# Mamba-style block with a top-2 expert FFN on one core: the same work in another order

## The chip, the cores and the metric

The kernel runs on one core of one Trainium2 chip. The metric is the device time of one execution in microseconds (us), lower is better. The core has five in-order instruction queues that matter here: TensorE (PE, with its weight loads PEld), VectorE (DVE), ScalarE (ACT), GpSimd (POOL) and SyncE (SP), which issues nearly all DMAs. They meet only at semaphores: an instruction that waits holds all that stands behind it on its own queue.

## What is computed

Batch 4, length 1024, width 1024, all float32. First a selective-scan block over the context (512 wide) is gated by the layer-normed input z, then an FFN with two of eight small experts a batch element.

```python
# block 1, per batch element; z = layernorm(x) taken with channels as the time axis
x1  = in_proj_w @ ctx;  u = silu(causal_conv4(x1) + conv_b)
x_dbl = x_proj_w @ u                      # 32 rows dt, 16 rows B, 16 rows C
delta = softplus(dt_proj_w @ dt + dt_proj_b);  A = -exp(A_log)
state = state * exp(delta*A) + (delta*u) * B   # a scan over 1024 steps, 16 states a channel
y = (sum_n state*C + D*u) * silu(z);  x = x + y.T
# block 2, with h = layernorm(x)
logits = h.reshape(b, -1) @ switch_w.T + switch_b   # 1M x 8 weights
gate, top = top_k(softmax(logits), 2)
o = sum over the 2 experts of gate * (gelu(h @ w1.T + b1) @ w2.T + b2), in 16 heads of 64
x = x + (h + o) @ w3.T + b3
```

## The kernel before

**Tiling and stages.** Time is cut in two halves of T = 512, channels in J = 8 blocks of P = 128. A batch has STEPS = 16 steps, one for a half and a channel block, and there are NB = 4 batches, so 64 steps (g = 0 to 63). A step has SLOTS = 8 slots, and in a slot two of the N = 16 states are done: slot t of a batch is step t // 8, q = t % 8. So a batch has slots 0 to 127. After the last comes a tail of its own slots (b = NB), which holds what is left of the FFN of the last batch.

**A slot.** ScalarE makes dA = exp(delta * A) for two states (L1246, a ring of RA = 4). VectorE makes the product du * B in PSUM (times_b, L1501) and scans (L1525) into h, which has RH = 3 pairs. POOL multiplies the pair by C (L865). TensorE adds the pair into yT by transposing matmuls (sum_pair, L962). In batch 0 ten of the sixteen du * B products run on TensorE instead (times_b, L948), out of duT, which is du_s turned by turn_du (L929, at q = 7) and copied by ScalarE at q = 0 of the next step (copy_duT, L1209).

**Once a step.** For the step AHEAD = J + 2 steps on: in_proj (L900, PE, q = 6, through PSUM bank S), first tap of the convolution (tap_one, ACT, L1163 to L1172, q = 1), three taps on VectorE between scans (tap, L1357), Silu (silu_u, L1178, q = 6). For the next step: v (dt_proj, L921, PE, q = 2), softplus on ScalarE (L1190 to L1196, q = 4) and its last part on VectorE (softplus_c, L1373, q = 3), du_s on POOL (L836), its copy (copy_du, L1202, ACT, q = 7). For the gate: xz normed (L1261, ACT, q = 3), turned (zT, L1081, PE, q = 4), Silu (L1278, q = 6, szT), szT times yT (L1425), added to xt on POOL (L852), stored.

**x_proj.** It is needed once for a half. It runs in the step with st % 8 == 6, four blocks at q = 6 and four at q = 7 (x_proj and x_proj_end, L912, bank S). split_rows (ACT, L1184 and L1185) takes its rows at the start of the next step, ahead of that step's first dA. In that step in_proj runs twice (slot 0 and slot 6), and everything from tap to v is a slot later. Steps 7 and 15 are such steps (in batch 3 only step 7).

**The FFN** of batch b - 1 is laid over the scan of batch b by a hand-written plan (class Schedule): the lists `slots[b][t]` say what every engine does in slot t beside the scan. `forward` places the work: logits (L1112), routing on VectorE (route1, route2), then for each half u of the time eight units hp: hidden (L1055, PE), gelu (L1331, ACT, with a table load before and one after, L1213), expert_out (L1065, PE), out_add (L1477, DVE). Units of half 0 start at slot 39 and those of half 1 at slot 83, one in two slots. Then 32 w3 tile parts a half (L1135, PE; four parts make a tile; a bias by L1131 at its start), evenly over slots 56 to 78 and 99 to 126, and tile_out (L1489, DVE, and the store on SP) two slots behind a tile's last part. renorm (L1310) and turn (L1042) make the normed rows and their transposes.

**LN1.** The scale r1 and shift nm1 of the next batch come from ln1_stats at slots 57 to 67 (ACT, L1300 to L1304), ln1_rstd (POOL, L806) at slot 124 and ln1_shift (DVE, L1366) at slot 126. ln1_rstd waits until the last xz of its batch is normed (zn_done), since there is one copy of r1.

**The tail** needs the last rows of x1 (late_row, SP, L702), their statistics (L1443), logits out of 32 switch tiles (sw_tail, SP, L734, of which 23 are loaded in the last slots of batch 3 and after), renorm, the selection of the experts, 16 units and 64 tiles.

Of the kernel before, what the change touches and what calls it, by code (L numbers as in the profile page):

```python
# [11 lines left out]
P = 128  # L12
# [13 lines left out]
HL = DC - 1  # L26
SD = 128
# [36 lines left out]
class Schedule:  # L64
# [32 lines left out]
    def add(self, b, t, *what):  # L97
        self.slots[b][t].append(what)

    def scan(self, b, rows):  # L100
# [12 lines left out]
        if b + 1 < NB:  # L113
            for k in range(J):
                rows.append((b, 54 + 3 * k // 2, "ln1", k))
                self.add(b, 57 + 3 * k // 2, "ln1_stats", k)
            self.add(b, 124, "ln1_rstd")
            self.add(b, 126, "ln1_shift")

    def forward(self, b, rows):  # L120
# [19 lines left out]
        for u, hidden, tiles, span in ((0, 39, 56, 23), (1, 83, 99, 28)):  # L140
# [7 lines left out]
            for dh in range(NQ):  # L148
                for k in range(TB):
# [4 lines left out]
                    self.add(b, at[m + W3C - 1] + 2 if at[m + W3C - 1] < 126 else 127, "tile_out", u, dh, k)  # L154
# [8 lines left out]
    def tail(self, rows):  # L163
        b = NB

        for m in range(SWL * TB):
# [4 lines left out]
            elif m < AFTER_B:  # L171
                self.add(b - 1, 114, "sw_tail", m)
        for q in range(PAIRS):
            self.add(b - 1, 120 + q, "sw_tail", AFTER_B + q)
            self.add(b - 1 if q < PAIRS - 1 else b, (121 + q) % 128, "sw_tail", AFTER_B + PAIRS + q)
        for m in range(AFTER_B + 2 * PAIRS, SWL * TB):
            self.add(b, 0, "sw_tail", m)
        for k in range(TB):
            self.add(b - 1, 126, "late_row", k)
        for k in range(TB):  # L180
# [10 lines left out]
            self.add(b, 10 + SWL * k + 8, "renorm", k)  # L191
# [6 lines left out]
        self.add(b, 45, "route2")  # L198
        for k in range(TB):
# [14 lines left out]
        for dh in range(NQ):  # L214
            for u in (0, 1):
                for k in range(TB):
# [3 lines left out]
                    self.add(b, t, "tile_out", u, dh, k)  # L220
# [42 lines left out]
def build(nc, x, ctxT, w_inT, conv_w, conv_b, x_projT, dt_projT, dt_b, A_log, D, sw, sw_b,  # L263
# [4 lines left out]
    with ExitStack() as ctx:  # L268
# [17 lines left out]
        minus_half = sb("minus_half", [P, 1])  # L286
# [33 lines left out]
        r1 = sb("r1", [P, J])  # L320
        nm1 = sb("nm1", [P, J])
# [18 lines left out]
        b1s = sb("b1s", [P, 1])  # L340
        b2s = sb("b2s", [P, 1])
# [27 lines left out]
        wt = sww[:, 0].rearrange("p e s -> p (e s)")[:, 0:E * HD].rearrange("p (e f) -> p e f", e=E)  # L369
# [87 lines left out]
        sel_step = sem("sel_step")  # L457
        renorm_done = sem("renorm_done")
# [89 lines left out]
        def hs_of(b, hp):  # L548
            return hs_tail if b == NB and hp % 2 else hs[:]

# [12 lines left out]
        def _(sync):  # L563
# [86 lines left out]
            def slot(b, t):  # L650
# [33 lines left out]
                for what, *a in PLAN.slots[b][t]:  # L684
# [50 lines left out]
                    elif what == "sw_load":  # L735
# [43 lines left out]
                    elif what == "tile_out":  # L779
                        uu, dh, k = a  # L780
                        n = part_index(b, uu, dh, k, 0) // W3C
                        lo = half(uu) * T + k * P
                        e.wait_ge(evac[bank_of(b, "tile", uu, dh, k)], 1 + count(b, "tile", uu, dh, k) + 1)
                        e.dma_start(out[b - 1:b, lo:lo + P, dh * QD:(dh + 1) * QD]
# [861 lines left out]
```

## Time and profile before

| | |
|---|---|
| runs | 2468.3, 2472.0, 2475.0 us; median 2472.0 |
| profiled execution | 2471.2 us, span 2469.3 us |
| PE busy | 2013.5 us, 82% |
| DVE busy | 2133.6 us, 86% |
| ACT busy | 1602.4 us, 65% |
| POOL busy | 1445.2 us, 59% |

Scans run from 78.9 to 2272.2 us, 64 steps; the tail follows. Steps of batch 0 take 26.3 to 40.8 us, the longest being steps 7 and 15; steps of batches 1 to 3 take 30.3 to 43.9. Batches 1, 2 and 3 start at 561.7, 1145.3 and 1727.0 us. A step's number in the text is st, its place in its batch.

Times in rows are microseconds from the span's start. "[1.10 <-ACT u L1172]" behind an instruction says that its engine was idle for 1.10 us before it, and that this instruction of ScalarE ended the wait. "issue" is a wait for which the profile shows no releaser. Several instructions of a kind are merged in a timeline row, with the count behind x.

### The profile page before, as it was taken

What the parts mean: (1) busy time and instruction counts of PE and PEld (TensorE: products, weight loads), DVE (VectorE), ACT (ScalarE), POOL (GpSimd) and SP (SyncE); (2) the same over time, 40 slices, a digit from 0 to 9 for tenths busy, and PEclk for the clock granted to TensorE, in tenths of its full rate; (3) what the DMA queues carried; (4) which work ended last, traced back from release to release, by engine and by line L of the source; (5) the groups of instructions that cost most, each with busy time, mean ns of one, the idle gap of its engine ahead of it and who ended that gap; (6) DMA issues with size and microseconds to landing.
All of it is one profiled execution on the core that took longest, in us unless ns stands there. A gap on an engine that the chain in (4) does not pass through costs nothing.

```text
span 2469.3 us, 32717 instructions
## 1 busy us (share of the span) xinstructions
PE 2013.5 (82%) x10776; PEld 1203.1 (49%) x10776; DVE 2133.6 (86%) x2712; ACT 1602.4 (65%) x2357; POOL 1445.2 (59%) x993
## 2 busy tenths in 40 slices
PE   6798888985757997996675897898685798797899
PEld 2677676653433553454453454454453455344344
DVE  5899789979999899998999899998999899999322
ACT  2677787656669868655667878855576857954500
POOL 0588677767756566566675566665775666665000
PEclk9899889997878998997888999899787899999899
DMA  5311434555612754566542464466460174578412
GB/s 174 128 37 52 150 99 148 188 162 169 246 37 103 261 166 133 161 204 203 188 155 74 140 232 152 147 224 199 154 239 26 60 253 145 164 251 283 168 56 72
DMA packets 200329, 383.01 MB, mean 155 GB/s; under 512 B 31553, under 2 KB 97089, under 8 KB 200162
## 3 DMA queue, kind: packets, MB, share of 16 engines
q1 hardware_dynamic: 196992, 380.47, 46.1%
q8 instruction: 86, 1.41, 0.2%
q10 hardware_dynamic: 3170, 0.47, 0.1%
q14 instruction: 81, 0.66, 0.1%
HBM read 346.80 MB, written 34.08 MB: 154 GB/s over the span
## 4 chain that ended last, share of the span: by engine, by line
PE 44%; DVE 19%; issue 17%; ACT 14%; POOL 3%; DMA 1%; DVEq 0%; SPq 0%; ACTq 0%; POOLq 0%
PE dense L1135 13%; PE dense L962 9%; DVE h L1525 9%; PE dense L900 5%; ACT dA L1246 4%; PE dense L948 3%; DVE dense L1501 3%; POOL h L865 3%; DVE u L1357 2%; PE dense L912 2%; PE dense L1112 2%; ACT L1213 2%; PE dense L921 2%; PE dense L1065 2%; PE dense L969 2%
## 5 line engine op out<-in xcount | busy, mean ns | idle before, releaser
L865 POOL TENSOR_TENSOR h<-h,Cb 128x1024 f32<-128x1024 f32 x512 | 1208.4, 2361 | 431.8 <-DVE h L1525 408.2
L1246 ACT ACTIVATE dA<-delta,Av 128x512 f32<-128x512 f32 x1024 | 703.1, 717 | 384.6 <-DVE h L1525 381.3
L962 PE MATMUL dense<-ident,h 128*128 128x128 f32 x4096 | 605.4, 299 | 165.0 <-POOL h L865 163.5
L962 PEld LDWEIGHTS dense<-ident,h 128*128 128x128 f32 x4096 | 521.1, 155 | 315.6 <-POOL h L865 225.8
L1525 DVE TENSOR_TENSOR_SCAN h<-dA,state,dense 128x512 f32<-128x512 f32 x512 | 627.4, 1263 | 31.0 <-issue 14.4
L1525 DVE TENSOR_TENSOR_SCAN h<-dA,dense 128x512 f32<-128x512 f32 x512 | 596.7, 1203 | 22.0 <-PE dense L962 8.5
L1501 DVE TENSOR_TENSOR dense<-dense,Bb 128x512 f32<-128x512 f32 x864 | 550.5, 682 | 1.6
L1135 PE MATMUL dense<-w3h,xT 128*128 128x512 f32 x832 | 386.0, 598 | 0.0
L859 POOL COPY state<-h 128x2 f32<-128x2 f32 x256 | 47.6, 186 | 336.6 <-DVE h L1525 335.1
L948 PE MATMUL dense<-Bb,duT 128*128 128x128 f32 x1280 | 179.9, 289 | 41.1 <-DVE h L1525 31.7
L1135 PEld LDWEIGHTS dense<-w3h,xT 128*128 128x128 f32 x832 | 147.9, 192 | 130.1 <-issue 130.1
L900 PE MATMUL dense<-ctxs,win 128*128 128x512 f32 x432 | 208.5, 628 | 2.2 <-ACT szT L1278 1.5
L948 PEld LDWEIGHTS dense<-Bb,duT 128*128 128x128 f32 x1280 | 160.4, 199 | 72.9 <-issue 65.6
L921 PE MATMUL dense<-dtaug,dtw 33*128 33x512 f32 x128 | 95.2, 832 | 110.2 <-DVE u L1357 108.5
L1357 DVE SCALAR_TENSOR_TENSOR u<-dense,cw,u 128x511 f32<-128x511 f32 (+2 forms) x192 | 140.7, 733 | 50.6 <-ACT u L1172 24.8
L1213 ACT ACT_TABLE_LOAD x113 | 145.0, 1283 | 2.0
L900 PEld LDWEIGHTS dense<-ctxs,win 128*128 128x128 f32 x432 | 84.2, 204 | 101.8 <-issue 101.8
L1112 PE MATMUL dense<-sww,row 128*32 128x256 f32 x1336 | 110.5, 417 | 1.2 <-ACT row L1287 1.2
L1065 PE MATMUL dense<-hs,w2s 128*64 128x512 f32 x224 | 72.8, 729 | 44.0 <-ACT hs L1331 41.4
L1202 ACT COPY dense<-du_s 128x512 f32<-128x512 f32 x64 | 37.5, 587 | 103.5 <-DVE dense L1501 103.3
L921 PEld LDWEIGHTS dense<-dtaug,dtw 33*128 33x128 f32 x128 | 24.5, 239 | 140.5 <-issue 140.4
L1487 DVE TENSOR_TENSOR res<-res,h 128x512 f32<-128x512 f32 x16 | 11.1, 691 | 88.1 <-PE dense L1135 88.1
(168 smaller groups left out, 2084.1 us busy)
## 6 DMA issues: line engine op xcount, KB each, us to landing
sww<-in_sw SPq DMA_DIRECT2D x167, 512.0 KB, 4.2
Cb<-bc_scratch SPq DMA_DIRECT2D x64, 512.0 KB, 6.1
Bb<-bc_scratch SPq DMA_DIRECT2D x54, 512.0 KB, 4.6
w3h<-in_sw SPq DMA_DIRECT2D x52, 512.0 KB, 8.2
w3h<-in_w3T SPq DMA_DIRECT2D x52, 512.0 KB, 5.2
row<-x_scratch SPq DMA_DIRECT2D x40, 512.0 KB, 4.5
xz<-in_x SPq DMA_DIRECT2D x64, 256.0 KB, 4.7
xt<-in_x SPq DMA_DIRECT2D x64, 256.0 KB, 3.9
```

The costliest lines, as they stand in the source:

```text
L865: e.tensor_tensor(h[:, s:s + 2, :], h[:, s:s + 2, :], Cb[:, 2 * q:2 * q + 2, :], ALU.mult).then_inc(prod_done, 1)
L900: mm = e.matmul(dense[:, bank, :], win[:, par, k, :], ctxs[:, k, :], start=(k == 0), stop=(k == DK - 1))
L921: e.matmul(dense[:, S, :], dtw[0:DR + 1, j * P:(j + 1) * P], dtaug[:], start=True, stop=True) \
L948: mm = e.matmul(dense[:, product_bank(g, n), k * P:(k + 1) * P], duT[:, g % 2, k, :], Bb[:, n, k * P:(k + 1) * P], start=True, stop=True)
L962: mm = e.matmul(yT[:, k, :], h[:, 2 * ((PAIRS * g + q) % RH) + i, k * P:(k + 1) * P], ident[:], is_transpose=True, start=False, stop=(q == ...
L1112: mm = e.matmul(dense[32 * n:32 * n + 32, F2, 0:32 * E], rows[:, lo:lo + 32], weights[:, :, 32 * n:32 * n + 32], start=first, stop=(k % TB ...
L1135: mm = e.matmul(dense[:, bank, :], xT_of(b, uu)[:, d, k * P:(k + 1) * P], w3[:, d, :], start=(b == NB and d == 0), stop=(d == J - 1), skip ...
L1213: e.preload_act_table_set("natural_log_exp_and_others")
L1246: e.activation(dA[:, i % RA, :], delta[:, st % 2, :], ACT.Exp, scale=Av[:, j * N + n:j * N + n + 1]).then_inc(dA_done, 1)
L1357: i = e.scalar_tensor_tensor(out=u[:, G % UR, s:T], in0=dense[:, bank, 0:T - s], scalar=cw[:, j, k:k + 1], in1=u[:, G % UR, s:T], op0=ALU. ...
L1501: e.tensor_tensor(dense[:, product_bank(g, n), :], du[:], Bb[:, n, :], ALU.mult).then_inc(duB_done, 1)
L1525: e.tensor_tensor_scan(h[:, 2 * ((PAIRS * g + q) % RH) + n % 2, :], dA[:, (N * g + n) % RA, :], dense[:, product_bank(g, n), :], state[:, ...
```

## The change

Only the order of the work changes, and two small buffers.

- split_rows moves behind the first two dA and uD of its step.
- x_proj's first half waits for four of the eight u, its second half for all. On ScalarE at q = 6, Silu of szT comes ahead of Silu of u.
- In batch 0 turn_du moves from the end of q = 7 to ahead of in_proj (or x_proj) at q = 6.
- hidden and its unit move one slot later, to 40 and 84; tiles to 57 to 78 and 100 to 126. tile_out may now fall in slot 128, which is slot 0 of the next batch.
- hidden waits only for w1s, expert_out and gelu for the whole selection. In the tail the second half of w1s is made on POOL (select), in steps of its own.
- ln1_rstd and ln1_shift move to slots 69 and 71; r1 and nm1 get two buffers.
- In batch 3 late_row moves from slot 126 to 125, and the switch tiles of slots 124 and 125 to 126. In the tail renorm moves from slots 18, 26, 34 and 42 to 33, 35, 46 and 46.

The diff, cut to its core:

```diff
     def add(self, b, t, *what):
+        if b < NB and t >= STEPS * SLOTS:
+            b, t = b + 1, t - STEPS * SLOTS
         self.slots[b][t].append(what)
...
-            self.add(b, 124, "ln1_rstd")
-            self.add(b, 126, "ln1_shift")
+            self.add(b, 69, "ln1_rstd")
+            self.add(b, 71, "ln1_shift")
...
-        for u, hidden, tiles, span in ((0, 39, 56, 23), (1, 83, 99, 28)):
+        for u, hidden, tiles, span in ((0, 40, 57, 22), (1, 84, 100, 27)):
...
-                    self.add(b, at[m + W3C - 1] + 2 if at[m + W3C - 1] < 126 else 127, "tile_out", u, dh, k)
+                    self.add(b, at[m + W3C - 1] + 2, "tile_out", b, u, dh, k)
...
+        for k in range(TB):
+            self.add(b - 1, 125, "late_row", k)
         for q in range(PAIRS):
-            self.add(b - 1, 120 + q, "sw_tail", AFTER_B + q)
-            self.add(b - 1 if q < PAIRS - 1 else b, (121 + q) % 128, "sw_tail", AFTER_B + PAIRS + q)
+            for t, m in ((120 + q, q), (121 + q, PAIRS + q)):
+                t = t if t < 124 else max(t, 126)
+                self.add(b - (t < 128), t % 128, "sw_tail", AFTER_B + m)
...
-        for k in range(TB):
-            self.add(b - 1, 126, "late_row", k)
...
-            self.add(b, 10 + SWL * k + 8, "renorm", k)
+            self.add(b, (33, 35, 46, 46)[k], "renorm", k)
...
+        self.add(b, 45, "select")
...
# gpsimd, ln1_rstd
-                e.wait_ge(zn_done, 1 + STEPS * b)
+                e.wait_ge(zn_done, 1 + STEPS * max(b - 1, 0))
...
# gpsimd, in the tail
+                    elif what == "select":
+                        e.wait_ge(top_step, 1 + 9 * (b - 1) + 8)
+                        e.wait_ge(experts_loaded, 1 + 64 * b)
+                        e.tensor_tensor(wt1, w12[:, 0], hot[:, 1, :].unsqueeze(2).broadcast_to([P, E, HD]), ALU.mult) \
+                            .then_inc(w1_step, 1)
+                        for n, rest in ((1, 4), (2, 2)):
+                            e.wait_ge(w1_step, 1 + n)
+                            e.tensor_tensor(wt1[:, 0:rest], wt1[:, 0:rest], wt1[:, rest:2 * rest], ALU.add).then_inc(w1_step, 1)
+                        e.wait_ge(w1_step, 1 + 3)
+                        e.tensor_tensor(w1s[:, 1, :], wt1[:, 0], wt1[:, 1], ALU.add).then_inc(w1_step, 1)
...
# tensor
-                e.wait_ge(u_done, 1 + J * (c + 1))
+                e.wait_ge(u_done, 1 + J * c + J // 2)
...
                     times_b_at(N * g + 2 * q + 3)
+                    if q == SLOTS - 2 and g + 1 < STEPS:
+                        turn_du(g + 1)
...
-                            e.wait_ge(sel_step, 1 + 9 * b)
+                            e.wait_ge(sel_step, 1 + selected(b) + (5 if b < NB else 3))
+                            if b == NB:
+                                e.wait_ge(w1_step, 1 + 4)
...
+                        if hp == 0:
+                            e.wait_ge(sel_step, 1 + selected(b + 1))
...
                     elif what == "x_proj_end":
+                        e.wait_ge(u_done, 1 + J * (c + 2))
                         x_proj_part(c + 1, range(J // 2, J))
...
-                if b == 0 and q == SLOTS - 1 and g + 1 < STEPS:
-                    turn_du(g + 1)
...
# scalar
-                if b < NB and late(b, t, 0) and st % J == J - 1 and c + 1 < NB * TH:
-                    split_rows(c + 1)
...
                         e.activation(uD[:], u[:, g % UR, :], ACT.Copy, scale=Dv[:, j:j + 1]).then_inc(uD_done, 1)
+                        if st % J == J - 1 and c + 1 < NB * TH:
+                            split_rows(c + 1)
...
                         e.wait_ge(x1_done, 1 + g)
+                        e.wait_ge(zT_done, 1 + g + 1)
+                        e.activation(szT[:].rearrange("p k e -> p (k e)"), dense[:, S, :], ACT.Silu) \
+                            .then_inc(evac[S], 1)
...
                             silu_u(G, S, last_step(b, st, "in_proj"))
-                        e.wait_ge(zT_done, 1 + g + 1)
-                        e.activation(szT[:].rearrange("p k e -> p (k e)"), dense[:, S, :], ACT.Silu) \
-                            .then_inc(evac[S], 1)
...
# vector, route2
-                for src, on, dst in ((w12[:, 0], hot[:, 0, :], w1s[:, 0, :]), (w12[:, 0], hot[:, 1, :], w1s[:, 1, :]),
-                                     (w12[:, 1], hot[:, 3, :], w2s[:])):
+                first = [(w12[:, 0], hot[:, i, :], w1s[:, i, :]) for i in ((0,) if b == NB else (0, 1))]
+                for src, on, dst in (*first, (w12[:, 1], hot[:, 3, :], w2s[:])):
```

## Rows read from the trace of the kernel before

**Rows 1.** Windows view, core 0: start:end, length, busy us of each engine (instructions), PEclk, DMA.

```profile
733.00:770.00 37.00, 25.39 (x121) 12.72 (x118) 33.67 (x42) 34.76 (x47) 22.80 (x19) 0.91 0.29 101
845.00:881.00 36.00, 34.95 (x140) 20.81 (x139) 33.74 (x41) 30.30 (x49) 21.60 (x11) 0.95 0.79 279
1063.00:1101.00 38.00, 38.00 (x185) 19.09 (x184) 32.54 (x39) 18.29 (x28) 23.31 (x15) 1.00 0.60 204
```

**Rows 2.** Waits of VectorE, whole span: who waits for whom, total us, times, longest.

```profile
DVE delta L1373 <- ACT delta L1196: 33.0, 16, 5.1
DVE h L1525 <- issue: 20.9, 8, 5.9
DVE h L1525 <- PE dense L962: 16.9, 26, 1.8
DVE h L1525 <- ACT dA L1246: 12.5, 11, 5.6
DVE res L1489 <- PE dense L1135: 11.5, 8, 2.5
```

**Rows 3.** Waits of all engines in 130 to 270 (batch 0).

```profile
DVE u L1357 <- ACT u L1172: 5.5, 5, 1.1
ACT duT L1209 <- PE dense L929: 4.8, 5, 1.0
```

**Rows 4.** Waits of VectorE in 427 to 492 (batch 0, steps 12 to 14).

```profile
DVE u L1357 <- ACT u L1163: 5.3, 3, 1.8
```

**Rows 5.** Timeline of PE from 424 and of DVE from 425: start, duration, instruction.

```profile
425.77 1.04 PE L962 MATMUL dense<-ident,h 128*128 128x128 f32 x8
...
427.01 2.45 DVE L1525 TENSOR_TENSOR_SCAN h<-dA,state,dense 128x512 f32<-128x512 f32 x2
```

**Rows 6.** Timeline of PE from 519, and waits of PE in the whole span.

```profile
519.24 0.66 PE L929 MATMUL dense<-ident,du_s 128*128 128x128 f32 x4
...
PE dense L948 <- ACT duT L1209: 5.2, 3, 1.8
```

**Rows 7.** Timeline of 1095.4 to 1102.6 (batch 0's FFN, into step 15 of batch 1).

```profile
1099.43 0.57 ACT L1184 COPY dtaug<-dense 32x512 f32<-32x512 f32 x1 [6.72 <-PE dense L912]
1101.44 1.28 DVE L1525 TENSOR_TENSOR_SCAN h<-dA,state,dense 128x512 f32<-128x512 f32 x1 [5.87 <-issue]
```

**Rows 8.** Waits of PE in 1001.6 to 1128.4.

```profile
PE dense L921 <- DVE u L1357: 3.0, 1, 3.0
```

**Rows 9.** Waits of DVE in 733 to 770.

```profile
DVE u L1357 <- ACT u L1172: 2.1, 1, 2.1
DVE h L1525 <- PE dense L962: 0.3, 1, 0.3
```

**Rows 10.** Lines view of ACT in 733 to 809: busy us, mean ns, idle before.

```profile
L1331 ACT ACT_TABLE_LOAD x8 | 10.3, 1283 | 3.9 <-PE dense L1055 3.9
```

**Rows 11.** Timeline of PE in 803.6 to 826.

```profile
822.50 0.60 PE L1131 MATMUL dense<-ident,b3c 128*128 128x128 f32 x4
822.94 1.88 PE L1135 MATMUL dense<-w3h,xT 128*128 128x512 f32 x4
824.75 1.12 PE L921 MATMUL dense<-dtaug,dtw 33*128 33x512 f32 x2
```

**Rows 12.** Timeline of PE from 2316: the first hidden pair of the tail.

```profile
2316.61 1.22 PE L1055 MATMUL dense<-xT,w1s 64*128 64x512 f32 x2 [2.92 <-DVE b2s L1599]
```

**Rows 13.** The instructions of L1366 (durations in ns), and one in DVE's timeline from 551.

```profile
L1366 DVE SCALAR_TENSOR_TENSOR nm<-mv,r x4: 137/2300/2306, 81.1 to 1714.9; 128x8 f32<-128x8 f32 x4
...
551.34 2.30 DVE L1366 SCALAR_TENSOR_TENSOR nm<-mv,r 128x8 f32<-128x8 f32 x1 [3.39 <-POOL r L806]
```

**Rows 14.** Timelines of PE and DVE in the tail.

```profile
2274.73 1.97 PE L962 MATMUL dense<-ident,h 128*128 128x128 f32 x8 [3.76 <-POOL h L865]
...
2278.97 0.67 DVE L1425 TENSOR_TENSOR szT<-dense,szT 128x512 f32<-128x512 f32 x1
...
2298.99 1.12 PE L1042 MATMUL dense<-ident,ctxs 128*128 128x128 f32 x8 [0.77 <-ACT xT L1320]
```

More of the change, by code:

```diff
@@ L26 @@
 HL = DC - 1
+SELECT = 9
 SD = 128
@@ L219, in tail @@
                         self.add(b, t, "tile", u, dh, k, c)
-                    self.add(b, t, "tile_out", u, dh, k)
+                    self.add(b, t, "tile_out", b, u, dh, k)
                     t += 4
@@ L285, in build @@
         iota = sb("iota", [P, E])
-        minus_half = sb("minus_half", [P, 1])
+        small = sb("small", [P, 3])
+        minus_half, b1s, b2s = small[:, 0:1], small[:, 1:2], small[:, 2:3]
         xpw = sb("xpw", [P, J, DR + 2 * N])
@@ L319, in build @@
         mv1 = sb("mv1", [P, J, 2])
-        r1 = sb("r1", [P, J])
-        nm1 = sb("nm1", [P, J])
+        r1 = sb("r1", [P, 2, J])
+        nm1 = sb("nm1", [P, 2, J])
         row = sb("row", [P, 2, DI])
@@ L368, in build @@
         xT_tail = u[:, UR - J:UR, :]
-        wt = sww[:, 0].rearrange("p e s -> p (e s)")[:, 0:E * HD].rearrange("p (e f) -> p e f", e=E)
+        wt, wt1 = [sww[:, 0].rearrange("p e s -> p (e s)")[:, i * E * HD:(i + 1) * E * HD].rearrange("p (e f) -> p e f", e=E)
+                   for i in (0, 1)]
         dense = ctx.enter_context(nc.psum_tensor("dense", [P, 8, T], F32))
@@ L457, in build @@
         sel_step = sem("sel_step")
+        w1_step = sem("w1_step")
         renorm_done = sem("renorm_done")
@@ L549, in hs_of, with selected @@
             return hs_tail if b == NB and hp % 2 else hs[:]
+        def selected(b):
+            return SELECT * (b - 1) if b <= NB else SELECT * NB - 2
         def part_index(b, uu, dh, k, c):
@@ L779, in slot @@
                     elif what == "tile_out":
-                        uu, dh, k = a
-                        n = part_index(b, uu, dh, k, 0) // W3C
+                        fb, uu, dh, k = a
+                        n = part_index(fb, uu, dh, k, 0) // W3C
                         lo = half(uu) * T + k * P
-                        e.wait_ge(evac[bank_of(b, "tile", uu, dh, k)], 1 + count(b, "tile", uu, dh, k) + 1)
-                        e.dma_start(out[b - 1:b, lo:lo + P, dh * QD:(dh + 1) * QD]
+                        e.wait_ge(evac[bank_of(fb, "tile", uu, dh, k)], 1 + count(fb, "tile", uu, dh, k) + 1)
+                        e.dma_start(out[fb - 1:fb, lo:lo + P, dh * QD:(dh + 1) * QD]
                                     .rearrange("o p d -> p (o d)"), res[:, n % 2]).then_inc(out_stored[n % 2], 16)
@@ L1260, in slot @@
                         e.wait_ge(xz_loaded, 1 + 16 * (g + 1))
-                        e.activation(xz[:], xz[:], ACT.Identity, scale=r1[:, j:j + 1], bias=nm1[:, j:j + 1]) \
+                        e.activation(xz[:], xz[:], ACT.Identity, scale=r1[:, b % 2, j:j + 1], bias=nm1[:, b % 2, j:j + 1]) \
                             .then_inc(zn_done, 1)
@@ L1479, in slot @@
                     elif what == "tile_out":
-                        uu, dh, k = a
-                        bank = bank_of(b, "tile", uu, dh, k)
-                        n = part_index(b, uu, dh, k, 0) // W3C
-                        e.wait_ge(part_done, 1 + part_index(b, uu, dh, k, W3C - 1) + 1)
+                        fb, uu, dh, k = a
+                        bank = bank_of(fb, "tile", uu, dh, k)
+                        n = part_index(fb, uu, dh, k, 0) // W3C
+                        e.wait_ge(part_done, 1 + part_index(fb, uu, dh, k, W3C - 1) + 1)
                         e.wait_ge(res_loaded[n % 2], 1 + 16 * (n // 2 + 1))
-                        if b == NB:
+                        if fb == NB:
                             e.wait_ge(b3_loaded, 1 + 16)
@@ L1558, in route2 @@
             def route2(b):
-                r, n = 5 * (b - 1), 9 * (b - 1)
+                r, n = 5 * (b - 1), selected(b)
                 e.wait_ge(pexp_done, 1 + b)
@@ L1597, in route2 @@
                                        b1s[:]).then_inc(sel_step, 1)
-                e.wait_ge(sel_step, 1 + n + 8)
+                e.wait_ge(sel_step, 1 + n + done + 1)
                 e.tensor_tensor_reduce(lgm[:, :, 0], b2c[:], rt[:, 4, :], 1.0, 0.0, ALU.mult, ALU.add,
                                        b2s[:]).then_inc(sel_step, 1)
-                e.wait_ge(sel_step, 1 + n + 9)
+                e.wait_ge(sel_step, 1 + n + done + 2)
             turns(slot)
```

10 lines of the change are left out of this document (4 added, 6 removed).

## The prediction

> **What bounds the kernel now.** I read the windows by stage first, because a share over the whole span mixes stages. In 733 to 770 (batch 1, step 5) VectorE and ScalarE are both near full, 33.7 and 34.8 of 37.0 us; in 845 to 881 and in 1063 to 1101 TensorE is full, 34.95 of 36 and 38.0 of 38 [rows 1]. So the limit changes: VectorE with a late ScalarE or TensorE input in batch 0, VectorE and ScalarE together while expert units run (steps 4 to 6 and 10 to 12 of batches 1 to 3), TensorE where w3 tiles run (steps 8 to 9 and 12 to 15). Next come VectorE's waits [rows 2]: 20.9 us before scans for "issue" and 12.5 for dA, 33.0 us for the last softplus activation, 16.9 us for the sums on TensorE, 11.5 us for w3 tiles. These are what an edit of order alone can give back; each is asked below for what is late next.
>
> **turn_du ahead of in_proj (batch 0).** In 130 to 270 ScalarE waits five times for the turned du (4.8 us), and VectorE five times 1.10 us for the first tap [rows 3]. The second follows from the first: ScalarE's queue is duT copy, uD, two dA, tap. Four us earlier on TensorE, du is turned before ScalarE asks, and the tap's wait goes: 1.10 in each of steps 1 to 6, 6.6 us. In steps 12 to 14 the same wait is 5.3 us in three [rows 4]. What is late next: in_proj and the pair sum behind it slip by one turning, 0.66 us [rows 6], and the next step's first scan needs that sum. It ends at 426.81 and the scan starts at 427.01 [rows 5], so about 0.5 is lost in each of these three: 3.8 stay. In steps 1 to 6 the same sum ends 0.9 us ahead of its scan, so nothing is lost. Sum 10.4; bounds 5 and 12. TensorE now waits for du_s ahead of in_proj; POOL makes it one product earlier than the sum behind it needs, so I count nothing.
>
> **split_rows behind the first dA.** At 1099.43 ScalarE takes the x_proj rows, for which it has waited, and the first dA, queued behind, lets VectorE stand 5.87 us until 1101.44 [rows 7]. dA, dA and uD can run in that wait, so this stall goes, in eight less one step changes. But the copies themselves start no earlier, for they wait for x_proj on TensorE, and from them run in_proj, taps, v, softplus. From 1001.6 to 1128.4 TensorE has one wait, 3.0 us for v at the start, and none after it [rows 8]: v of step 15 stands in a full TensorE queue. VectorE then reaches softplus_c earlier and waits there longer. In steps 15 of batches 1 and 2 I count 0 of the 5.87. In batch 0 TensorE waits three times for the duT copy, 5.2 us [rows 6]; the two longest, 1.77 each, stand behind the split of steps 7 and 15, and both go: 3.5 us. The bounds are 0 and the whole stalls (rivals). The first half of x_proj no longer waits for the last u and szT's Silu comes first: 0.6 us where TensorE waits there, 0 where it is full; counted 0.
>
> **Expert units one slot later, tiles 57 to 78 for 56 to 78, and 100 to 126 for 99 to 126.** A unit is two table loads of 1.28 us [rows 10] and two gelus on ScalarE. The gelus leave slots 0, 2, 4, 6 of a step for 1, 3, 5, 7.
> Step 5: gelu now stands behind the tap, so the tap's 2.1 and the 0.3 for a sum go [rows 9]; softplus now stands behind the gelu of slot 3, and worked through in order from the piece lengths of this step its last part ends about 0.6 after VectorE arrives: 1.8 net, three batches, 5.4 us. Bounds: minus 1.8 (in the following step, where I work the same chain from a full ScalarE: 0.3 for the tap, 1.2 for out_add and dA behind the gelu of slot 7, 1.8 at softplus_c, 3.3 in all against 3.3 now, so 0) and plus 2.4 a step.
> Step 7: in_proj to v holds five tile parts now: three together and two of 1.88 each, as at 822.94; v starts at 824.75 [rows 11]. With tiles from slot 57 only three parts stand before v, and one bias of 0.60 less: 4.3 us of queue with starts overlapping 0.5, so 3.8. Against it the last gelu, then the split, stands ahead of in_proj: 1.0 later. 2.8 in each of three batches, 8.4 us; bounds 0 and 3.8, the softplus wait being 3.5.
> Step 8: a tile_out at slot 65 waits 2.2 in batches 1 and 2 (within the eight waits of 11.5 us [rows 2]) and moves on one slot. TensorE has 36.00 less 34.95 to give [rows 1]: 1.0, 1.0, and 0.5 in batch 3, 2.5 us.
> Steps 12 to 15: as many tile parts (28) stand between v of slot 98 and v of slot 123 as before, but the last hidden pair now comes behind the first v: 1.22 a pair [rows 12], 1.1 net. In the full queue that is lost twice: minus 2.2. Steps 10 and 11: 0.
> Sum 14.1; it is the least certain term, bounds minus 8 and 20.
>
> **LN1 scale at slots 69 and 71.** Its product on VectorE takes 0.137 us once and 2.30 three times; before it VectorE waits 3.39 in batch 0 [rows 13] and 0.99 twice, 5.4 in all. The second buffer removes the wait for the last xz, and the waits of 5.4 go. The 2.30 is only moved, since POOL runs its products there too. In batch 0 it costs in step 8 what it gave in step 15: 3.4 net. In batches 1 and 2 it lands where TensorE is full and VectorE waits 1.8 for a sum right behind [rows 2], so all but 0.5 is covered: 0.99 + 2.30 - 0.5, 2.8 each. Sum 9.0; if the cover fails, 5.4. The trace shows that the 2.30 us product ends with POOL's product, not when its own work is done. The Trainium skill (SBUF — State Buffer, SBUF: two separate sides) has an exclusive lock on the port pair that VectorE, with two SBUF inputs, and GpSimd share, "the other fully blocks"; by it moving work to POOL beside VectorE is no free gain, and the trace agrees with the 2.30.
>
> **tile_out over the batch's end, tail.** The last tile_out leaves slot 127, where it waits, for the next slot 0, after its tile is done. The three waits at batch ends are 4.2 of the 11.5 us [rows 2], and 0.7 of its own work leaves the path to the last product: 4.9 us; bounds 2 and 5.
> late_row goes ahead of four switch tiles on SP. Now the sum ends at 2274.73 + 1.97 = 2276.70 and szT's product starts at 2278.97 [rows 14], held by the rows' statistics: 2.3 us. Behind late_row on SP stand its wait for the stored x1, the xt load and the moved switch tiles of 512 KB; these are used over 10 us after they land now, so nothing is added. Renorm no longer stands ahead of xT's copy: 0.8 at 2298.99 [rows 14]. The first hidden waits 2.92 for the whole selection [rows 12]; now it waits for w1 alone, but two renorms stand ahead of the turned copies and hold the turns on TensorE. Between 0 and 2.9; I take 0.5, since two renorms are 2.3 to 2.5. Sum 3.6.
>
> **The sum.** 10.4 + 3.5 + 14.1 + 9.0 + 4.9 + 3.6 = 45.5 us off the profiled execution's 2471.2 (span 2469.3 and 1.9 around it; the runs' median is 2472.0): 2425.7, on the median's scale 2426. About 0.3%, 7.4 us, is what a measurement of this kernel can tell from no change.
>
> **Rivals.** (1) The expert units give nothing: the longer waits at softplus_c, out_add and first dA take back what taps and tiles give. For it: ScalarE has 34.8 us of work in a step of 37 already [rows 1]. Against: the two fewer parts before v are plain work. 2471.2 - 31.4 = 2440; at minus 8 it is 2448. 0.22.
> (2) The stalls at the first scans are gone in full, because TensorE catches up: 4.9 + 5.6 in batch 0 (in the 12.5 for dA), 2.2 three times and 5.9 twice (18.3 of the 20.9 for issue [rows 2]), 28.8 us, of which 3.5 and 8.4 are counted: 16.9 more, 2409. Against it is the queue without a wait [rows 8]. 0.12.
> (3) Slower: a gelu in an odd slot stands behind du's copy or xz, expert_out waits for it in TensorE's queue in order, and the pair sums, v and x_proj_end wait behind expert_out. There are 48 units; the other terms give 31.4, so it decides from 0.65 us a unit, and above 0.81 the kernel is slower by over 0.3%. ScalarE already waits 3.9 us in eight units for hidden [rows 10], 0.5 a unit. At 1.1 a unit: 2471.2 - 31.4 + 52.8 = 2493. Against it: TensorE has idle time in these steps, so its waits are mostly free. 0.04.
> Within 0.3%, by several halves failing: 0.04. Forecast 0.58.
>
> **How the numbers follow.** Faster 0.58 + 0.22 + 0.12 = 0.92, same 0.04, slower 0.04. The range reaches from rival 2 (2408) to rival 1 at its bound and a failed half of the turn_du term, 2452.
>
> **What would show it.** Batch 0: steps 2 to 6 at 26.1 for 27.2 us and no wait of the duT copy (L1209). Step 15 of batches 1 and 2: no wait at the first scan, but one of 8 us or more at softplus_c. Step 7: v 3 us earlier behind its in_proj, softplus wait under 2. No wait before nm, its 2.30 kept. Steps 5 and 6: waits at softplus_c instead of at the tap. I am wrong if the sum of steps 5 and 6 is over 76.4 us (as now), or if the softplus_c wait of step 15 stays at 3.4.

## The result and the profile after

| | before | after |
|---|---|---|
| median of five runs (lowest to highest), us | 2469.7 (2468.3 to 2475.0) | 2455.6 (2451.2 to 2457.7) |
| ratio, 95% interval | | 0.9937 (0.9921 to 0.9953) |
| profiled execution, its span, us | 2471.2, 2469.3 | 2454.4, 2452.4 |
| batch 0, first scan to first scan of batch 1 | 482.8 | 460.0 |
| batch 1 | 583.7 | 586.3 |
| batch 2 | 581.7 | 585.2 |
| batch 3 | 545.2 | 549.3 |
| from the last scan to the end | 197.0 | 192.1 |

The kernel is faster by 14.1 us, 0.6%. Forecast were 45.5 us, 2426 with a range from 2408 to 2452: the sign is right and the time is outside. Among the kernels of the experiments three (split alone, hidden first, units old) had one far slower execution each (2568, 2565 and 4809 us), which is not in the ratios and moves the medians by at most 0.4 us. The lower five lines of the table are differences of times in the timeline of VectorE (starts of scans, and the end of the last), and they show at once where the forecast failed. Batch 0 gave 22.8 us, more than the 17.3 that its terms promised (10.4 for turn_du, 3.5 for the split, 3.4 for LN1). Batches 1 to 3, from which the rest was to come, are 10.2 us longer.

VectorE's waits, whole span of the kernel after (who waits for whom: us in total, times, longest), the lines that answer to [rows 2]. L1399 is softplus_c, L1503 out_add, L1551 the scan, L1515 tile_out:

```profile
DVE delta L1399 <- ACT delta L1222: 45.3, 21, 4.0
DVE xT L1503 <- PE dense L1092: 45.2, 20, 5.4
...
DVE h L1551 <- PE dense L983: 18.1, 27, 1.8
...
DVE res L1515 <- PE dense L1161: 10.0, 7, 4.0
...
DVE h L1551 <- ACT dA L1270: 7.8, 9, 3.5
DVE h L1551 <- issue: 3.3, 3, 1.8
```

The waits of the scans fell as the change means them to: "issue" from 20.9 to 3.3, dA from 12.5 to 7.8. Against that softplus_c rose from 33.0 to 45.3, and out_add, which waits for expert_out, rose to 45.2. In the same view of before it is already the largest of these waits behind softplus_c's, and neither [rows 2] nor the prediction's list of VectorE's waits names it:

```profile
DVE xT L1477 <- PE dense L1065: 28.0, 21, 7.0
```

The windows that answer to [rows 1], in the kernel after: step 5 and step 14 of batch 1 (us of PE, PEld, DVE, ACT, POOL, then the granted clock, DMA share and GB/s):

```profile
710.80:750.60 39.80, 28.50 (x114) 14.98 (x112) 33.64 (x43) 32.52 (x44) 24.36 (x19) 0.79 0.27 94
...
1047.80:1080.60 32.80, 32.71 (x161) 16.91 (x160) 32.77 (x40) 18.56 (x28) 22.32 (x15) 1.00 0.73 251
```

Step 14 fell from 38.8 to 32.8: VectorE goes straight into step 15 instead of standing at its first scan. Step 5 rose from 37.0 to 39.8, though VectorE has the same work in it (33.64 for 33.67) and ScalarE 2.2 us less. Something between the engines got longer, and the next view shows it. Timeline of step 5 in the kernel after (start, duration, instruction, idle before it); L1080 is hidden, L921 in_proj, L1357 the gelu with its table load, L1092 expert_out:

```profile
739.35 5.39 PE L921 MATMUL dense<-ctxs,win 128*128 128x512 f32 x8 [0.25 <-ACT szT L1299]
744.67 1.13 PE L1080 MATMUL dense<-xT,w1s 64*128 64x512 f32 x4
745.88 1.28 ACT L1357 ACT_TABLE_LOAD   x1 [2.12 <-PE dense L1080]
748.53 1.08 PE L1092 MATMUL dense<-hs,w2s 128*64 128x512 f32 x4 [1.71 <-ACT hs L1357]
749.65 0.75 DVE L1503 SCALAR_TENSOR_TENSOR xT<-dense,small,xT 128x512 f32<-128x512 f32 x1 [3.16 <-PE dense L1092]
```

The hidden pair of slot 46 stands right behind in_proj of slot 46 on TensorE. ScalarE waits for it, expert_out waits for ScalarE, out_add for expert_out, and VectorE stands 3.16 us. The last out_add of step 6 (batch 1) has a wait of 5.09 of the same kind: its hidden pair, of slot 54, stands behind the first half of x_proj (L933) and its expert_out, of slot 55, behind the second:

```profile
779.66 5.66 PE L933 MATMUL dense<-u,xpw 128*64 128x512 f32 x8 [0.24 <-ACT szT L1299]
785.25 1.13 PE L1080 MATMUL dense<-xT,w1s 64*128 64x512 f32 x4
787.34 3.22 PE L933 MATMUL dense<-u,xpw 128*64 128x512 f32 x7
...
791.90 0.75 DVE L1503 SCALAR_TENSOR_TENSOR xT<-dense,small,xT 128x512 f32<-128x512 f32 x1 [5.09 <-PE dense L1092]
```

In step 5 of the kernel before, the pair that was needed next had left TensorE before in_proj began, and in_proj ran beside the gelu:

```profile
756.36 1.13 PE L1055 MATMUL dense<-xT,w1s 64*128 64x512 f32 x4
760.67 3.67 PE L900 MATMUL dense<-ctxs,win 128*128 128x512 f32 x8 [0.57 <-ACT szT L1278]
761.83 1.28 ACT L1331 ACT_TABLE_LOAD   x1
765.61 0.75 DVE L1477 SCALAR_TENSOR_TENSOR xT<-dense,b2s,xT 128x512 f32<-128x512 f32 x1 [0.66 <-PE dense L1065]
```

In_proj itself took 5.39 us in the kernel after and 3.67 in this one, which is the clock; the last section comes back to it.

### The profile page after: what moved, and what is told of

It reads as the page before. It is cut to its first block, busy times and chain, and to the rows that moved or that the text cites. A ratio compares the mean times of both kernels' runs of the same rounds, so it can differ in the third digit from the quotient of the medians.

```text
span 2452.4 us, 32732 instructions
## 1 busy us (share of the span) xinstructions
PE 2013.3 (82%) x10776; PEld 1202.3 (49%) x10776; DVE 2132.7 (87%) x2710; ACT 1602.3 (65%) x2357; POOL 1449.0 (59%) x997
## 4 chain that ended last, share of the span: by engine, by line
PE 33%; DVE 23%; issue 22%; ACT 18%; POOL 4%; DVEq 1%; DMA 0%; ACTq 0%; POOLq 0%; SPq 0%
DVE h L1551 11%; PE dense L1161 10%; PE dense L983 5%; ACT dA L1270 5%; DVE dense L1527 5%; PE dense L921 4%; POOL h L876 3%; ACT L1239 3%; PE dense L1080 3%; PE dense L969 2%; DVE u L1383 2%; PE dense L933 2%; PE dense L1138 2%; PE dense L990 2%; ACT hs L1357 2%
## 5 line engine op out<-in xcount | busy, mean ns | idle before, releaser
L1551 DVE TENSOR_TENSOR_SCAN h<-dA,state,dense 128x512 f32<-128x512 f32 x512 | 628.8, 1268 | 22.8 <-PE dense L983 10.9
L1551 DVE TENSOR_TENSOR_SCAN h<-dA,dense 128x512 f32<-128x512 f32 x512 | 597.3, 1205 | 11.5 <-PE dense L983 7.2
L921 PE MATMUL dense<-ctxs,win 128*128 128x512 f32 x432 | 211.0, 634 | 10.7 <-ACT szT L1299 9.5
L921 PEld LDWEIGHTS dense<-ctxs,win 128*128 128x128 f32 x432 | 84.8, 206 | 110.8 <-issue 110.8
L1092 PE MATMUL dense<-hs,w2s 128*64 128x512 f32 x224 | 70.1, 680 | 65.3 <-ACT hs L1357 64.8
L1080 PE MATMUL dense<-xT,w1s 64*128 64x512 f32 x224 | 85.5, 752 | 8.4 <-DVE xT L1503 8.4
```

The source lines that it names most:

```text
L921: mm = e.matmul(dense[:, bank, :], win[:, par, k, :], ctxs[:, k, :], start=(k == 0), stop=(k == DK - 1))
L1080: e.matmul(dense[:, bank, :], w1s[HD * i:HD * i + HD].rearrange("p k f -> p (k f)"), xT_of(b, uu)[HD * i:HD * i + HD, hp, :], start=True, ...
L1551: e.tensor_tensor_scan(h[:, 2 * ((PAIRS * g + q) % RH) + n % 2, :], dA[:, (N * g + n) % RA, :], dense[:, product_bank(g, n), :], state[:, ...
```

## The experiments

The theory formed on these rows: the expert units' new slots cost what the other parts gave, through two orders, hidden behind in_proj on TensorE, and softplus behind a gelu on ScalarE. The rival is the prediction's own term, by which the slots give 14.1 us and something else failed. Ratios are against runs of the kernel before on the same chip (its medians there were 2469.2 to 2470.7). The intervals of the ratios are 2 to 5 us to either side, so a difference of medians between two of these kernels is good to some microseconds and no better. What a step took is far steadier: outside steps 5, 6 and 10, and batch 0, steps whose order two kernels share mostly agree to 0.1 us. The table of all twelve, and then each:

| kernel | median us | ratio (95%) |
|---|---|---|
| slots alone | 2505.0 | 1.0158 (1.0139 to 1.0178) |
| after, slots old | 2436.5 | 0.9863 (0.9848 to 0.9877) |
| turn_du alone | 2456.3 | 0.9946 (0.9933 to 0.9959) |
| split alone | 2465.2 | 0.9979 (0.9970 to 0.9988) |
| after, hidden first | 2431.0 | 0.9846 (0.9826 to 0.9866) |
| after, units old, tiles new | 2425.9 | 0.9825 (0.9806 to 0.9845) |
| after, LN1 at 124 and 126 | 2460.2 | 0.9960 (0.9946 to 0.9974) |
| after, softplus first | 2434.2 | 0.9861 (0.9844 to 0.9877) |
| after, both first | 2424.0 | 0.9818 (0.9802 to 0.9835) |
| after, units old, tiles 57 and 99 | 2417.2 | 0.9794 (0.9777 to 0.9810) |
| the same, softplus first | 2416.2 | 0.9784 (0.9768 to 0.9800) |
| after, tile_out capped at slot 127 | 2468.7 | 0.9994 (0.9985 to 1.0004) |

**The slots alone, and all but the slots.**

```diff
-        for u, hidden, tiles, span in ((0, 39, 56, 23), (1, 83, 99, 28)):
+        for u, hidden, tiles, span in ((0, 40, 57, 22), (1, 84, 100, 27)):
```

> The kernel before with the expert units (40, 84) and the w3 tiles (57 to 78, 100 to 126) in their new slots, nothing else. Theory 1 (the prediction's term): 14.1 us faster, steps 5, 7 and 8 of batches 1 to 3 shorter by 1.8, 2.8 and 0.8. Theory 2 (new, from the trace after): in slot 46 and 86, 94 the hidden pair now stands right behind in_proj on TensorE, so the gelu behind it and out_add come late; slots cost about 15 us in all (steps 5 to 13 of the three batches are 5.0, 5.0 and 5.3 longer once the moved LN1 product's 2.3 is taken off), more if the split gave step 7 its gain: 2485 to 2492.

> The kernel after with the expert units and tiles back in the slots of before (39, 56 to 78; 83, 99 to 126), all else kept. Theory 1: 14.1 us slower than after, about 2469. Theory 2: 15 to 20 us faster than after, 2436 to 2440, with the waits of out_add for expert_out back from 45.2 us to about 28.

Alone, the slots cost 34.3 us by the medians and 39 by the ratio (34 to 44). Theory 1 had them 14.1 us faster, and even the 2485 to 2492 of theory 2 were too low. Taken out of the change, they leave it at 2436.5, 19.1 us faster than after. Both directions contradict the prediction's term, and the second has about the time that rival (1) gave a change whose slots are worth nothing (2440). VectorE's waits in the kernel with the slots alone, and in the one without them:

```profile
DVE xT L1477 <- PE dense L1065: 56.6, 20, 5.9
DVE delta L1373 <- ACT delta L1196: 47.6, 27, 5.1
```

```profile
DVE delta L1399 <- ACT delta L1222: 32.3, 10, 5.4
DVE xT L1503 <- PE dense L1092: 31.0, 25, 5.4
```

That the same edit costs more alone than in company has one known place, step 7. Alone it shortens that step by 3.6, 3.6 and 0.5 us in batches 1 to 3. Put on top of the rest it shortens it by 6.0, 7.3 and 1.3, since there the moved split has left a wait of 5.4 at softplus_c, which fewer w3 parts ahead of v take away. That is 6.7 us in the three batches. By the steps of the profiled executions the edit cost 28.8 alone and 16.1 in company; the rest of that difference is spread over the other steps in pieces of up to 2.4.

**Units and tiles apart.** The line above with (0, 39, 57, 22), (1, 83, 100, 27) in the kernel after: units old, tiles new.

> The kernel after with the expert units back at 39 and 83 and the w3 tiles at their new slots (57 to 78, 100 to 126). Against the kernel with both back (2436.5): the prediction has 2.8 us in each step 7 of three batches from the tiles, two parts fewer ahead of v; then it is 2428, with softplus_c's wait of 5.4 in step 7 down to about 2. If the gain in step 7 of the new slots came from the units and not from the tiles, it stays at 2436.

2425.9, so the units' slot costs 29.7 us against after, and the tiles' slots give 10.7 against both old. The step at which the prediction looked for it shows it. Waits of VectorE in step 7 of batch 2, first with both old, then with the tiles new:

```profile
DVE delta L1399 <- ACT delta L1222: 5.4, 1, 5.4
```

```profile
DVE delta L1399 <- ACT delta L1222: 1.7, 1, 1.7
```

But in step 12 of batches 1 and 2 tile_out now waits 4.4 and 2.9, because the second half's tiles start at 100. This asks for the next kernel.

**The second half's tiles back at 99.** (0, 39, 57, 22), (1, 83, 99, 28) in the kernel after.

> The kernel after with the units back at 39 and 83, the first half's tiles at their new slots (57 to 78) and the second half's back at 99 to 126. Against units old and all tiles new (2425.9), whose step 12 waits 4.4 and 2.9 us for w3 tiles in batches 1 and 2: these waits go, and step 7 keeps its gain: 2418 to 2421. If the second half's tiles give it back in step 15, 2426.

2417.2. VectorE's wait in step 12 of batch 1, with the tiles from 100:

```profile
DVE res L1515 <- PE dense L1161: 4.4, 1, 4.4
```

With the tiles from 99 it is not there, step 7 keeps its gain, and nothing comes back in step 15, which is 1.4 and 1.0 us shorter than after's in batches 1 and 2.

**Why the units lose: hidden behind in_proj.**

```diff
-                self.add(b, t, "hidden", u, hp)
+                self.slots[b][t].insert(0, ("hidden", u, hp))
```

> The kernel after with each hidden pair ahead of in_proj and v in its slot on TensorE (it matters in slots 46, 86 and 94, where in_proj is, and 42, 50, 90, 98, where v is), nothing else. If the new slots lose because a gelu waits for a hidden pair behind in_proj (5.4 us of TensorE), out_add's waits for expert_out fall from 45.2 to below 32 us and the kernel is 8 to 12 us faster than after, 2443 to 2447. If they lose because softplus now stands behind a gelu, it stays within 3 us of after.

24.6 us faster than after, though no work is taken away: a hidden pair only changes places with in_proj or v where its slot has one (and, which the expectation leaves out, with x_proj in slot 54 and with zT in slots 44, 52, 84 and 92). This is also more than the 8 to 12 us expected. The same stretch of step 5 (this step is 35.0 long; after's is 39.8):

```profile
734.80 2.08 PE L1080 MATMUL dense<-xT,w1s 64*128 64x512 f32 x4
736.80 4.27 PE L921 MATMUL dense<-ctxs,win 128*128 128x512 f32 x8
740.35 1.28 ACT L1357 ACT_TABLE_LOAD   x1
744.12 0.75 DVE L1503 SCALAR_TENSOR_TENSOR xT<-dense,small,xT 128x512 f32<-128x512 f32 x1 [1.06 <-PE dense L1092]
```

ScalarE waits for nothing before its gelu, and out_add waits 1.06 for 3.16. The expectation named out_add's waits as the mark, below 32 in all; they fell only to 39.6. What else fell is softplus_c's, from 45.3 to 29.9. So the mechanism is shown at its place, and I had taken its effect to be all in one wait when it is in two. In step 5 softplus_c's wait falls from 1.9 to 0.3 in each batch; I put that down to the pair ahead of v, which frees the gelu ahead of softplus, but v, zT and in_proj were not tried apart.

**Softplus behind the gelu.**

```diff
-                    if q == 4 and g + 1 < ALL:
+                    if q == (4 if j == J - 1 else 3) and g + 1 < ALL:
                         e.wait_ge(du_s_done, 1 + g)
                         softplus_a(g + 1, (st + 1) % 2)
```

> The kernel after with softplus's activations in slot 3 of a step, ahead of the gelu there, instead of slot 4 behind it (not in steps 7 and 15). If the softplus behind the gelu is a part of the loss, softplus_c's waits of 1.9 in steps 5 and 6 and 1.6 to 3.5 in steps 11 and 12 go: 8 to 15 us faster than after. If the gelu is only pushed further and out_add waits in its place, nothing, or some us slower.

21.4 us faster than after, again more than expected. Waits of VectorE in steps 5 and 6 of batch 1, in the kernel after and in this one:

```profile
DVE xT L1503 <- PE dense L1092: 8.2, 2, 5.1
DVE delta L1399 <- ACT delta L1222: 3.8, 2, 1.9
```

```profile
DVE xT L1503 <- PE dense L1092: 4.8, 2, 3.4
DVE h L1551 <- PE dense L983: 2.0, 2, 1.0
```

Softplus_c's wait is gone and out_add's did not grow in its place, as the rival had it; over the whole span out_add's waits stay at 45.7. (Its fall in the lines above is of this batch alone: in steps 5 and 6 of batch 2 it waits 7.1 and 6.9, and in step 11 of batches 1 and 2 it waits 1.7 longer.)

> The kernel after with both edits of order: hidden ahead of in_proj and v on TensorE, and softplus in slot 3 ahead of the gelu. Each alone gave 24.6 and 21.4 us against after. If they are two causes, the sum is 2410 to 2415; if both shorten the same chain (hidden, gelu, softplus, dA), the second adds little: 2425 or more.

Together 31.6 us against after, nearer to the second expectation: the softplus edit adds 6.9 us to the hidden edit, where alone it gave 21.4. Most of what each frees is the same chain. They bring the new slots to 2424.0, where the old slots with the same tiles are at 2425.9: in sum, mending the two orders gives back as much as the units' slots cost. It does not give it back in the same places. Lengths of steps, batches 1 to 3 together, in us:

| step | 5 | 6 | 10 | 11 |
|---|---|---|---|---|
| cost of the units' slots (after less units old, tiles new) | 3.8 | 9.4 | 6.9 | 8.5 |
| given back by both orders (after less both first) | 14.1 | 7.5 | 3.7 | 1.9 |

In step 5 the mended order is far better than the old slots (34.7 in each batch, against 37.1 to 38.6 with the units back); in step 11 most of the loss stays and its cause is open. In step 6 the rest has a place. The last expert_out, of slot 55, still stands behind x_proj's second half, and out_add waits 2.8 to 3.5 in the three batches; batch 1:

```profile
777.39 3.22 PE L933 MATMUL dense<-u,xpw 128*64 128x512 f32 x7
...
781.96 0.75 DVE L1503 SCALAR_TENSOR_TENSOR xT<-dense,small,xT 128x512 f32<-128x512 f32 x1 [3.12 <-PE dense L1092]
```

So the two orders are a shown part of what the units' slots cost, not the whole of it, and that the sums agree is in part luck. (Hidden first with the old slots was not tried.) The counter-check is the softplus edit where no gelu stands in slot 3:

> As the last, and softplus in slot 3. With the units in their old slots no gelu stands in slot 3, so softplus was not behind one; then this changes nothing (within 3 us of the last), which is what the theory of softplus behind the gelu says. If softplus is late for another reason it is 8 us faster or more.

2416.2 for 2417.2: no difference that these runs tell, as expected.

**turn_du alone.** The move of turn_du to q = 6, on the kernel before.

> The kernel before with turn_du moved ahead of in_proj in batch 0, nothing else. The prediction's term: 10.4 us faster, 2459.3; steps 2 to 5 at 26.1. Rival from the trace after, where these steps take 25.2: it also takes away the waits for softplus and for the pair sum, 2.0 a step and not 1.1, and gives 16 us or more.

14.4 us, above the term of 10.4 and its bound of 12. VectorE's waits in steps 1 to 6, in 101 to 270 of before and in 101 to 255 here:

```profile
DVE u L1357 <- ACT u L1172: 6.6, 6, 1.1
DVE delta L1373 <- ACT delta L1196: 3.5, 5, 1.0
DVE h L1525 <- PE dense L962: 3.5, 7, 0.8
```

```profile
DVE h L1525 <- PE dense L962: 1.7, 6, 0.3
DVE u L1357 <- ACT u L1172: 0.2, 1, 0.2
```

The taps' 6.6 went as forecast, and with it all of softplus_c's 3.5, and that second part is the clock. In before, step 2 had the tap's wait of 1.1 and no wait for softplus, at a granted clock of 1.00 throughout; it gained 1.07, just the forecast. In steps 3 to 5 the clock was at 0.50 for 3.4 us, where TensorE does the sums ahead of v, softplus_c waited 0.5 to 0.7, and these steps gained 2.0 to 2.1. With the split alone, whose order here is that of before, step 1 kept its clock and had no such wait, and step 2 did not and had it (0.5). With turn_du moved the clock stayed at 1.00 in all of steps 1 to 6. The stretch ahead of v in step 3, before and here (PE, PEld, DVE, ACT, POOL, clock):

```profile
165.00:168.00 3.00, 2.81 (x13) 2.49 (x13) 3.00 (x5) 1.68 (x3) 2.07 (x3) 0.50 0.00 0
```

```profile
159.90:162.80 2.90, 2.64 (x15) 1.72 (x16) 2.90 (x4) 1.57 (x3) 1.98 (x3) 1.00 0.00 0
```

Steps 2 to 5 take 25.2 where 26.1 was forecast; step 1 gave 3.6, of which the split alone, which leaves its order as it is, also gave 2.6; steps 8 to 10 gave 1.3 back.

**The split alone.** split_rows behind the first dA and uD, on the kernel before.

> The kernel before with split_rows behind the first dA and uD, nothing else. The prediction's term: 3.5 us, all in batch 0; in step 15 of batches 1 and 2 the first scan's 5.9 returns in full at softplus_c. Rival (2) of the prediction: all 28.8 us go. From the trace after I expect something between: the stalls of 2.2 in step 7 of batches 1 to 3 go for good (step 7 falls by 2.3 to 35.7 less 2.3), and in step 15 the first scan's wait of 5.9 goes while softplus_c waits no longer than now (3.4 against 3.6 after): 10 to 20 us.

5.5 us; the term was 3.5. In batch 0 it gave 5.0, in batch 2 0.1, in batch 3 0.3; batch 1 is 1.4 longer, and the tail, which the edit does not touch, 2.5 shorter. My guess after seeing the trace, that step 7's gain stays, was wrong and the prediction was right: in batch 2 steps 6 and 14 are 2.3 and 6.0 shorter, and steps 7 and 15 are 2.3 and 6.0 longer. Waits of VectorE in step 15 of batch 2 and before its first scan, before and here:

```profile
DVE h L1525 <- issue: 5.9, 1, 5.9
DVE delta L1373 <- ACT delta L1196: 3.4, 1, 3.4
DVE res L1489 <- PE dense L1135: 1.1, 1, 1.1
...
```

```profile
DVE res L1489 <- PE dense L1135: 4.2, 2, 3.1
DVE delta L1373 <- ACT delta L1196: 3.6, 1, 3.6
DVE h L1525 <- PE dense L962: 1.5, 1, 1.5
...
DVE szT L1425 <- PE dense L962: 0.9, 1, 0.9
```

5.9 went; 3.1 came at w3 tiles, 1.5 and 0.9 at sums and 0.2 at softplus_c. With TensorE's queue full, it doesn't matter at which of its results VectorE stands.

**LN1 undone.** ln1_rstd and ln1_shift back at 124 and 126 in the kernel after, buffers kept.

> The kernel after with ln1_rstd and ln1_shift back at slots 124 and 126 (two buffers kept, so that there is no wait for the last xz). The prediction's term D splits in two: the waits of 5.4 us go by the second buffer, the product of 2.30 us on VectorE is covered in step 8 by 1.8 (batches 1 and 2). In steps 8 of after it was not covered, they are 2.3 longer. So moving it back gives 2.3 in each step 8 and costs 2.3 in each step 15: no change within 2 us in batches 1 and 2; in batch 0 too. If the place decides, it is 4 us or more to either side.

4.6 us slower than after; the intervals of the two ratios overlap, the steps do not leave it in doubt. I had read the 2.3 us longer step 8 of after as the cover failing. It did not: undoing the move shortens step 8 by 2.3 and lengthens step 9 by 2.2 in batches 1 and 2, so VectorE only stands later for the same full TensorE, and step 15 pays 3.0 and 3.4. The edit answers a second question too, which I had taken for settled. The two buffers were kept, and still VectorE waits for r in its old place as long as in before (3.39, 0.99 and 0.99 there; 3.40, 0.99 and 1.00 here):

```profile
DVE nm L1392 <- POOL r L817: 5.4, 3, 3.4
```

So the wait was not for the last xz, and the second buffer by itself takes none of it away. POOL goes from its other work straight into ln1_rstd and makes r in 1.66 us; in slots 69 and 71 VectorE gets there later than r, except in batch 0.

**tile_out held in slot 127.** The old rule, "+ 2 if at[...] < 126 else 127", in the kernel after.

> The kernel after with the last tile_out of a batch held in slot 127, as before, instead of slot 0 of the next batch; nothing else. The prediction's term: 4.9 us slower than after, with waits of VectorE for a w3 tile (L1515) in step 15 of batches 1, 2 and 3 longer by 2.5, 1.1 and 0.6 and each step 15 longer by 0.7 of its own work (which the next step loses).

13.1 us slower than after, not 4.9. Steps 15 of batches 1 to 3 are 2.8, 4.9 and 1.3 longer, 8.9 in all; 4.9 more are in step 6, whose order the edit doesn't touch (last section). The capped tile_out waits 3.1, 4.8 and 0.6 in batches 1 to 3. It waited 2.5, 1.1 and 0.6 in before, 1.3, 1.3 and 0.6 with the slots alone, and 1.3, 1.1 and 0.6 with the split alone. The last w3 part is in slot 126 with either start of the tiles, so these are not the reason. What is gone from the slot ahead of it on VectorE is ln1_shift, with a wait of 0.99 and a product of 2.30 in batches 1 and 2; the two terms share this place, and that the longer wait comes from it is argued, not tried.

## Why the prediction was wrong

**Expert units (14.1 forecast off, 19.1 to 34.3 on).** This is the step that failed. "Softplus now stands behind the gelu of slot 3 ... its last part ends about 0.6 after VectorE arrives" measured 1.9, in step 5 and in step 6. For the following step it says "1.2 for out_add and dA behind the gelu of slot 7, ... 3.3 in all against 3.3 now, so 0": out_add waited 5.1 there and 3.2 in step 5 itself. I worked the chain through on ScalarE alone, from its piece lengths, and put the hidden pair in as done. I never asked what the pair is queued behind in its new slot: in_proj in slots 46, 86 and 94, x_proj in slot 54. In step 5 putting it ahead gave 3.1 to 5.2 us a batch. The change moves sixteen units a batch on three queues, and the piece that decides is the one on TensorE, in the slot that also has in_proj. The mark set down for it did what it was meant to: the sum of steps 5 and 6, 76.4 before, is 81.8 in batch 1 and 79.6 in batch 2 (in batch 3 it is 77.9, where before had 78.2). The other mark, softplus_c's wait of step 15 staying at 3.4, came true as well, with 3.6.

**The rivals.** Rival (1) named the waits that grew, softplus_c and out_add, and its time at the bound, 2448, is the nearest; but it lets them take back only what taps and tiles give, and they took 19.1 us more. Rival (3), at 0.04, is the one in which the slots cost more than that. By its own count of 48 units it measured 19.1 / 48 = 0.40 us a unit for units and tiles together, and 0.62 for the units alone, under its threshold of 0.65. Its place was mostly wrong: it has pair sums, v and x_proj behind expert_out, and the trace has hidden behind in_proj and x_proj, and expert_out behind x_proj. Its sentence, "TensorE has idle time in these steps, so its waits are mostly free", is the same fault as above: idle in the sum of the step, full in slot 6.

**Tiles (8.4 and 2.5 in the term).** Right in mechanism: two parts fewer ahead of v shorten step 7, by 5.4, 6.6 and 2.9 against the kernel with old slots, 14.9 for 8.4. The start at 100 loses 4.6 and 2.9 in step 12 when the units are in their old slots, where I had put the tiles at 0 (the minus 2.2 was for a hidden pair). Step 8's 2.5 is not there in batches 1 and 2: tile_out's wait of 2.2 went, and in after the first tap waits 2.2 in its place.

**turn_du (10.4 forecast, 14.4 measured).** Right in mechanism and mis-sized: step 2 gave the 1.1 of the forecast and steps 3 to 5 gave 2.0 to 2.1, since with the edit TensorE kept its clock there. The steps 12 to 14 gave 4.3 for 3.8.

**The split (3.5 forecast, 5.5 measured).** Right in its main statement: batch 0 gives, batches 2 and 3 give nothing, and rival (2)'s 16.9 us more are not there. Wrong in where it comes back in step 15: "one of 8 us or more at softplus_c" is 3.6 in after, and the rest stands at w3 tiles.

**LN1 (9.0 forecast).** Half of it was there: undoing the place costs 4.6, waits included, for in the old place the waits of 5.4 come back though both buffers are kept. "The second buffer removes the wait for the last xz, and the waits of 5.4 go" is wrong in its reason. In the trace after, the wait is 0.9 once for 3.4, 0.99 and 0.99. The product still takes 2.3 us in its new place.

```profile
L1392 DVE SCALAR_TENSOR_TENSOR nm<-mv,r x4: 147/2255/2317, 81.7 to 1441.5; 128x8 f32<-128x8 f32 x4
```

**tile_out and tail (4.9 and 3.6).** The first is 8.9 by steps 15, with LN1 moved; what it is worth in the kernel before was not tried. The tail of the four kernels whose tail is the old one takes 194.2 to 197.0 us, that of the kernels with the new one 190.2 to 192.1: 4.1 between the means, for 3.6.

Without the units and tiles my terms made 31.4 us, and the kernel without them measured 34.2 (2470.7 less 2436.5). The error that decides is one term, of the wrong sign. That the others agree so well in sum is in part luck: one by one they measured 14.4 for 10.4, 5.5 for 3.5, 4.6 for 9.0, 8.9 for 4.9 and 4.1 for 3.6.

## What to carry to other kernels

When a piece of work moves one slot in a hand-written order, write down for each queue that it uses what stands directly ahead of it in the new slot: TensorE idle for 31% of step 5 in the kernel before was no cover for a pair that landed behind eight matmuls. Two moves that look like one (here units and tiles) are to be costed and tried apart; this change with the units left where they were, and the second half's tiles too, is 38 us faster than the whole of it, 2417 for 2456. And where TensorE's queue was full, removing a stall of VectorE moved the stall, and the next edit that shortened that queue was paid for both (step 7).

## What the runs showed of the hardware

The clock of TensorE is a price of its own in these traces, and it is not the same from batch to batch. Step 5 has the same order in batches 1 and 3 of the kernel after. In batch 1 in_proj's eight matmuls took 5.39 us; in batch 3:

```profile
1910.88 3.67 PE L921 MATMUL dense<-ctxs,win 128*128 128x512 f32 x8 [0.42 <-ACT szT L1299]
...
1919.46 0.75 DVE L1503 SCALAR_TENSOR_TENSOR xT<-dense,small,xT 128x512 f32<-128x512 f32 x1 [1.47 <-PE dense L1092]
```

The windows around the two in_proj, with the granted clock third from the end:

```profile
739.30:744.80 5.50, 5.45 (x10) 2.21 (x12) 5.50 (x7) 3.63 (x5) 4.23 (x3) 0.68 0.00 0
1910.80:1914.60 3.80, 3.72 (x10) 1.56 (x12) 3.80 (x6) 3.07 (x4) 2.77 (x3) 1.00 0.00 0
```

At 1.00 (2.4 GHz) throughout in_proj took 3.67; at a mean of 0.68, so 1.2 GHz for a good part of it, 5.39. Before both TensorE had waited for gelus and products; in batch 3 the clock was back just before in_proj, in batch 1 only during it. Out_add's wait is 3.16 in the one and 1.47 in the other, and the step 39.8 and 38.1 long. So of step 5's 2.8 us over before in batch 1 about 1.7 is clock, by the difference between the two batches, and the rest is order; this is an estimate, since before's own step 5 is 37.0 in batch 1 and 39.3 in batch 3. That is also the scatter of steps 5, 6 and 10 between kernels that agree there, up to 2.6 us a step, and why a sum over steps of one trace can be read to a few us only. In the whole span TensorE was busy 2013.3 us with its 10776 matmuls in after, at a mean granted clock of 0.904, and 1991.7 with the same 10776 where the units are back and the tiles new, at 0.913. So part of the 29.7 us that their slots cost came as clock; how much of these 21.6 us lay on the path is not known, and whether the order would still cost 29.7 us at a full clock was not tried.
